# Key-side sums of a random-feature attention with the values stationary, in column halves

## The reference, cut to what matters

```python
logits = jnp.einsum('bhld,hdf->bhlf', k, W0) - 0.5 * jnp.sum(k * k, axis=-1, keepdims=True)
alpha = jax.nn.softmax(logits.reshape(B, H, L * NF), axis=2).reshape(B, H, L, NF)
N = jnp.einsum('bhlf,bhld->bhfd', alpha, v)      # the key-side sums
D = jnp.sum(alpha, axis=2)                       # their denominators
phi = jax.nn.softmax(jnp.einsum('bhld,hdf->bhlf', q, W0), axis=-1)
num = jnp.einsum('bhlf,bhfd->bhld', phi, N)
den = jnp.einsum('bhlf,bhf->bhl', phi, D)
out = num / (den[..., None] + EPS)
```

## Time and profile before

| | |
|---|---|
| median of 3 runs | 1093.77 us (1092.8 to 1097.36) |
| the profiled execution | 1093.86 us, of which the span 1092.1 |
| TensorE matmuls busy | 1010.6 us, 93% of the span |
| TensorE weight loads busy | 783.5 us, 72% |
| VectorE busy | 742.9 us, 68% |
| ScalarE busy | 451.5 us, 41% |
| GpSimd busy | 219.8 us, 20% |
| chain that ended last | TensorE 73%, VectorE 13%, issue 6%, ScalarE 3% |
| mean granted TensorE clock | 0.977 |

### The profile page before, as it was taken

How to read it: one execution, slowest core, us unless ns; L and a number is a source line. 1 busy time by engine, 2 the same in 40 slices (tenths; PEclk the granted TensorE clock), 3 DMA queues, 4 the chain that set the end, 5 groups by cost and what they waited for, 6 DMA issues and landing times.

```text
span 1092.1 us, 15333 instructions
## 1 busy us (share of the span) xinstructions
PE 1010.6 (93%) x5740; PEld 783.5 (72%) x5740; DVE 742.9 (68%) x1277; ACT 451.5 (41%) x757; POOL 219.8 (20%) x179
## 2 busy tenths in 40 slices
PE   6889999999999989889898998999999999899998
PEld 3568778887665556788874886888765556568898
DVE  5646677557466766888858385874665676677776
ACT  4414454020555565344333254521235465454442
POOL 6101211224311011223200022211360011021110
PEclk9988999999999999999999899999999999899999
DMA  6101000211000000010010000011110000001111
GB/s 210 43 20 40 1 1 1 58 38 41 20 1 1 1 1 1 20 40 20 21 58 1 20 20 1 2 27 52 39 39 1 1 1 1 0 1 40 27 32 40
DMA packets 12926, 26.75 MB, mean 24 GB/s; under 512 B 2581, under 2 KB 7285, under 8 KB 12853
## 3 DMA queue, kind: packets, MB, share of 16 engines
q1 hardware_dynamic: 12852, 25.77, 7.8%
HBM read 23.51 MB, written 2.10 MB: 23 GB/s over the span
## 4 chain that ended last, share of the span: by engine, by line
PE 73%; DVE 13%; issue 6%; ACT 3%; POOL 2%; SPq 2%; DMA 1%; DVEq 0%; ACTq 0%; POOLq 0%
PE ps L1204 14%; PE ps L897 13%; PE ps L1125 10%; PE ps L1085 4%; PE ps L1040 4%; PE ps L1101 3%; PE ps L1025 3%; PE ps L1169 3%; PE ps L905 3%; PE ps L1170 3%; DVE wide_lo L849 3%; PE ps L1154 2%; PE ps L1015 2%; PE ps L999 2%; SPq L264 2%
## 5 line engine op out<-in xcount | busy, mean ns | idle before, releaser
L1204 PE MATMUL ps<-expert_hi,wide_hi 128*128 128x256 f32 x512 | 148.0, 289 | 19.4 <-DVE wide_lo L849 19.3
L1125 PE MATMUL ps<-region 128*128 128x512 f32 (+3 forms) x384 | 163.9, 511 | 0.0
L777 DVE TENSOR_REDUCE region<-ps 128x1 f32<-128x512 f32 (+1 forms) x192 | 100.6, 552 | 91.1 <-PE ps L1104 90.3
L1204 PE MATMUL ps<-expert_lo,wide_hi 128*128 128x256 f32 x512 | 144.4, 282 | 0.0
L1204 PE MATMUL ps<-expert_hi,wide_lo 128*128 128x256 f32 x512 | 144.0, 281 | 0.0
L301 POOL TENSOR_TENSOR expert_lo<-expert,expert_hi 128x1024 fp32r<-128x1024 f32 x32 | 81.4, 2544 | 264.3 <-ACT expert_hi L402 264.0
L561 ACT ACTIVATE region<-ps 128x512 f32<-128x512 f32 x192 | 92.7, 488 | 97.1 <-PE ps L1172 63.9
L402 ACT ACTIVATE wide_hi<-region 128x512 fp32r<-128x512 f32 x128 | 80.2, 630 | 119.1 <-DVE region L834 118.6
L809 DVE COPY_PREDICATED region<-region,ps 128x512 f32<-128x512 uint32 x112 | 80.9, 735 | 62.9 <-PE ps L897 62.5
L1204 PEld LDWEIGHTS ps<-expert_hi,wide_hi 128*128 128x128 f32 x512 | 96.9, 189 | 31.1 <-DVE wide_lo L849 25.3
L834 DVE TENSOR_TENSOR region<-ps,region 128x512 f32<-128x512 f32 x128 | 87.9, 689 | 38.6 <-PE ps L1154 38.2
(11 more groups left out here) (141 smaller groups left out, 1922.1 us busy)
## 6 DMA issues: line engine op xcount, KB each, us to landing
expert<-in_value_experts SPq DMA_DIRECT2D x16, 512.0 KB, 3.7
expert<-in_output_experts SPq DMA_DIRECT2D x16, 512.0 KB, 3.6
out<-X SPq DMA_DIRECT2D x8, 256.0 KB, 2.4
X<-in_x SPq DMA_DIRECT2D x2, 512.0 KB, 4.6
X<-in_x SPq DMA_DIRECT2D x1, 1024.0 KB, 9.9
W<-in_W SPq DMA_DIRECT2D x1, 512.0 KB, 7.0
expert<-in_W3q SPq DMA_DIRECT2D x1, 512.0 KB, 3.5
expert<-in_W3k SPq DMA_DIRECT2D x1, 512.0 KB, 3.5
```

The lines of the kernel that those rows point to most:

```text
L777: dve.tensor_reduce(mx[:, i, at_mx:at_mx + 1], ps[:, max_bank(h, m), 0:w], AX.X, ALU.max).then_inc(sem["s_max"], 1)
L1125: mm(ps[:, SUM_BANK[c], lo:CH], V3[:, j, h // 2, h % 2 * HD3:(h % 2 + 2) * HD3], PT[:, g % RING, lo:CH], start=(j == 0), stop=(j == TC * ( ...
L1204: last = mm(ps[:, 4 + t // 2, t % 2 * D:(t % 2 + 1) * D], r[:, m % MO, k * P:(k + 1) * P], w[:, g % SLOTS, p * D:(p + 1) * D], start=(n == ...
```

## The change

The two operands change places. For a pair p and tile t, 64 columns of `V1_all` (the pair's 34 and what follows them) are stationary and the 128 columns of `E1` move. The result is transposed: values on partitions, features along the row. Even pairs go to partitions 0 to 63 of bank 4, odd pairs to 64 to 127 (`v` in the code), alternating tile by tile, so all 8 pairs fit in one bank. ScalarE copies that bank to `N1T` once both halves are done (`n_sb`), ahead of the first copy to `phT`. In step 2, behind the transposes of tile 1, TensorE transposes it back with four transposes (`nT_ps`, bank 5); VectorE copies from there to `N1w`, now with 6 copies (three runs of pairs with the same window offset, two head positions), behind the max and subtraction of tile 2. L1006's products and L695's additions follow, each moved behind other work of their step.

```diff
--- before.py
+++ after.py
@@ -130,6 +130,8 @@
         k_max = view(H1)
 
         N1w = view(PAIRS1 * WIN).rearrange("p (k w) -> p k w", k=PAIRS1)
+        at[0] = 0
+        N1T = view(CH)
         at[0] = 5 * 1024
         cx = view(2 * D).rearrange("p (i n) -> p i n", i=2)
         cxT = view(2 * DA * P).rearrange("p (i a s) -> p i a s", i=2, a=DA)
@@ -168,7 +170,7 @@
             var_ready=3 * TT, rstd_ready=3 * TT, xn_ready=3 * TT, xnT_ps=3 * TT, xT_ready=3 * TT, bias_added=2 * TT,
             k_ps=2 * NC, k_sb=2 * NC, q_ps=2 * NC, q_sb=2 * NC, v_ps=TT, v_sb=TT, kk_sb=1, kk_ps=1,
             fk_ps=TT, mk_ready=DA * TT, fk_sub=TT, e_ready=TT, ak_top_ready=1, k_max_ready=1, ak_ready=1, w_ready=1, wv_ready=1,
-            n_ps=2, n_blk=2 * PAIRS1, za_ps=1, n_ready=3,
+            n_ps=2, n_sb=1, nT_ps=1, n_blk=6, za_ps=1, n_ready=3,
             f_ps=2 * TT, top_ready=2 * TT * DA, f_sub=2 * TT, f_exp=2 * TT, fT_ps=2 * TT, fT_sb=2 * TT,
             num_ps=2 * TT, cx_ready=2 * TT, cxT_ps=2 * TT, cxT_sb=2 * TT, y_ps=2 * TT,
             q2_ps=2 * NC, q2_sb=2 * NC,
@@ -468,10 +470,11 @@
                 for s in range(LAST):
                     if s in (2, 3):
                         piece_high(b, s - 2)
+                    if s == 1:
+                        until(act, "n_ps", b, 2)
+                        copy(N1T, ps[:, 4, :], "n_sb")
                     for a, t in due(s, 1):
                         until(act, "fT_ps", b, a * TT + t + 1)
-                        if a + t == 0:
-                            until(act, "n_ps", b, 2)
                         if t >= 2:
                             until(act, "num_ps", b, a * TT + t - 1)
                         i = t % 2
@@ -688,12 +691,6 @@
                 for s in range(LAST):
                     if s - 2 in GATES_AT:
                         gates(GATES_AT.index(s - 2))
-                    if s == 2:
-                        until(dve, "za_ps", b, 1)
-                        for k0, k1, w0 in N1_RUNS:
-                            dens = N1w[:, k0:k1, w0 + HD1:w0 + 2 * V1W:V1W]
-                            dve.tensor_tensor(dens, dens, ps[:, 6, 2 * k0:2 * k1].rearrange("p (a i) -> p a i", i=2),
-                                              ALU.add).then_inc(sem["n_ready"], 1)
                     for a, t in due(s, 0):
 
                         i = t % 2
@@ -713,17 +710,21 @@
                                                      m[:, q].unsqueeze(3).broadcast_to([P, 2, H // 4, F]),
                                                      ALU.subtract)
                         last.then_inc(sem["f_sub"], 1)
-                    if s == 1:
-
-                        until(dve, "n_ps", b, 2)
+                    if s == 2:
+
+                        until(dve, "nT_ps", b, 1)
                         until(dve, "windows_clear", b, 1)
-                        for k in range(PAIRS1):
-                            w0 = k * 2 * V1W - N1_at(k)
-                            n1 = ps[:, 4 + k // 4, k % 4 * P:k % 4 * P + 2 * V1W]
-                            dve.tensor_copy(N1w[0:HALF, k, w0:w0 + V1W], n1[0:HALF, 0:V1W]
+                        nT = ps[:, 5, :].rearrange("p (k w) -> p k w", w=HALF)
+                        for k0, k1, w0 in N1_RUNS:
+                            dve.tensor_copy(N1w[0:HALF, k0:k1, w0:w0 + V1W], nT[0:HALF, k0:k1, 0:V1W]
                                             ).then_inc(sem["n_blk"], 1)
-                            dve.tensor_copy(N1w[HALF:P, k, w0 + V1W:w0 + 2 * V1W], n1[HALF:P, V1W:2 * V1W]
+                            dve.tensor_copy(N1w[HALF:P, k0:k1, w0 + V1W:w0 + 2 * V1W], nT[HALF:P, k0:k1, V1W:2 * V1W]
                                             ).then_inc(sem["n_blk"], 1)
+                        until(dve, "za_ps", b, 1)
+                        for k0, k1, w0 in N1_RUNS:
+                            dens = N1w[:, k0:k1, w0 + HD1:w0 + 2 * V1W:V1W]
+                            dve.tensor_tensor(dens, dens, ps[:, 6, 2 * k0:2 * k1].rearrange("p (a i) -> p a i", i=2),
+                                              ALU.add).then_inc(sem["n_ready"], 1)
                     for a, t in due(s, 2):
 
                         i = t % 2
@@ -1000,12 +1001,6 @@
                                           W0[r, i, cols_of] if a == 0 else kblk[r, b, i, cols_of],
                                           start=True, stop=True)
                         last.then_inc(sem["f_ps"], 1)
-                    if s == 2:
-                        until(pe, "n_blk", b, 2 * PAIRS1)
-                        for k0, k1, w0 in N1_RUNS:
-                            last = mm(ps[:, 6, 2 * k0:2 * k1], eps_blk,
-                                      N1w[:, k0:k1, w0 + HD1:w0 + 2 * V1W:V1W], start=True, stop=True)
-                        last.then_inc(sem["za_ps"], 1)
                     for a, t in due(s, 1):
                         until(pe, "f_exp", b, a * TT + t + 1)
                         until(pe, "fk_sub", b, TT)
@@ -1015,15 +1010,27 @@
                             last = pe.transpose(ps[0:r, k // TC, k % TC * P:(k % TC + 1) * P],
                                                 phi[:, t % 2, k * P:k * P + r], ident)
                         last.then_inc(sem["fT_ps"], 1)
+                    if s == 2:
+                        until(pe, "n_sb", b, 1)
+                        for u in range(PAIRS1 // 2):
+                            last = pe.transpose(ps[:, 5, u * P:(u + 1) * P], N1T[:, u * P:(u + 1) * P], ident)
+                        last.then_inc(sem["nT_ps"], 1)
+                        until(pe, "n_blk", b, 2 * len(N1_RUNS))
+                        for k0, k1, w0 in N1_RUNS:
+                            last = mm(ps[:, 6, 2 * k0:2 * k1], eps_blk,
+                                      N1w[:, k0:k1, w0 + HD1:w0 + 2 * V1W:V1W], start=True, stop=True)
+                        last.then_inc(sem["za_ps"], 1)
                     if s < 2:
 
                         until(pe, "e_ready", b, TT)
                         until(pe, "wv_ready", b, 1)
-                        for p in range(s * PAIRS1 // 2, (s + 1) * PAIRS1 // 2):
+                        for u in range(s * PAIRS1 // 4, (s + 1) * PAIRS1 // 4):
                             for t in range(TT):
-                                c0 = (t * PAIRS1 + p) * 2 * V1W
-                                last = mm(ps[:, 4 + p // 4, p % 4 * P:p % 4 * P + WIN], E1[:, t, p * P:(p + 1) * P],
-                                          V1_all[:, c0:c0 + WIN], start=(t == 0), stop=(t == TT - 1))
+                                for v in range(2):
+                                    c0, p = (t * PAIRS1 + 2 * u + v) * 2 * V1W, 2 * u + v
+                                    last = mm(ps[v * HALF:(v + 1) * HALF, 4, u * P:(u + 1) * P],
+                                              V1_all[:, c0:c0 + HALF], E1[:, t, p * P:(p + 1) * P],
+                                              start=(t == 0), stop=(t == TT - 1))
                         last.then_inc(sem["n_ps"], 1)
                     for a, t in due(s, 2):
                         until(pe, "fT_sb", b, a * TT + t + 1)
```

## The result

The changed kernel takes 1077.39 us (median of 4 runs, 1075.85 to 1080.7), the kernel before 1094.17 us (4 runs, 1092.8 to 1097.36). The ratio is 0.9847, with a 95% interval of 0.9815 to 0.9878: faster by 1.5%, 16.8 us. The forecast was 1081 with a range of 1077 to 1096 and 0.68 for "faster". The direction and the mechanism held; the gain is 4 us larger than the 12.6 us of the sum.

What follows compares the result with a forecast made beforehand. The key-side sums on TensorE were taken to lie nearly all on the path. From 1093.9 us, 14.2 less for paired records and 1.6 more for the handover gave 1081.3, say 1081 us, range 1077 to 1096.

Steps and rivals of the forecast that it cites:

- the sum: Whole kernel: 14.2 us saved on the key-side sums, 1.6 lost at the handover, from 1093.9 to 1081.3 us.
- What bounds the stage: Key-side sums (L1025) lie nearly all on the path, about 33 us of the 1092.1 us span.
- What a record cost before: Second half of L1025: 0.113 us each, paced by the 128-column weight load, not the 102 moving columns.
- Two halves at the same time: Key-side sums: records in different column halves overlap, 0.0575 us each; second half 3.7 us, saving 3.5 per batch.
- The first rival: Key-side sums: column halves don't overlap, 0.107 to 0.113 us per record; total near 1095 us; chance 0.21.
- the 0.090 of the short group: Key-side sums only partly paired: 0.090 us per record, as in a short row-half group; total 1087.2 us; chance 0.08.
- 15.1 us for perfect pairs: Key-side sums: saving if each record costs 0.053 us, half of 107 ns.
- Bare loads: Key-side sums: loads come into the open and halves don't overlap, 0.163 us per record; total 1108.5 us; chance 0.08.
- The first halves: First 64 records of the sums per batch: 6.0 and 6.7 us, saving 3.6 each, slow time kept at 4.9 and 6.3.
- The handover: From T (start of L999 after the sums) to next L999: 10.0 us against 9.2, +1.6 in all.

Runs made afterwards that it cites:

- experiment 5: The kernel before with 34 or 68 moving columns instead of 102: 1116.42 us beside 1089.54, and 1107.29 us beside 1096.69.
- thin_load: The changed kernel with 34 stationary columns instead of 64 for seven of the eight tiles: 1079.49 us beside 1092.52 for the kernel before.
- filler: The changed kernel with two unused float32 matmuls in TensorE's idle time before the first half of the sums: 1075.59 us beside 1096.69 for the kernel before.
- same_half: The changed kernel with all key-side sums on output partitions 0 to 63, odd pairs in bank 5: 1091.71 us beside 1089.54 for the kernel before.
- Experiment 6: The changed kernel again, 1077.75 us, and with the way back ahead of tile 1's transposes and tile 2's max, 1075.98 us.
- even_only: The changed kernel without the odd pairs' sums but for their first tile, 36 records per half: 1072.53 us beside 1089.54 for the kernel before.

## Why the prediction was right, point by point

*What bounds the stage.* Right. The sums lay on the path: 15.88 us in the stage, 16.0 at the end, though that match is closer than the parts outside the stage (+1.0, +0.5 and -1.6 us) give a right to. I had expected these parts unchanged.

*What a record cost before.* Right: the moving columns don't set the 0.113 us. With 34 and 68 instead of 102 the records cost the same at the same clock (experiment 5). That it is the load is what is left; no run shortened the load alone in the old form.

*Two halves at the same time.* Right, shown from both sides: 7.13 us without different halves, 3.64 for 36 records as for 64. The first rival predicted a second half of 6.9 to 7.2; it is exactly what the kernel does once the halves are the same. The term was 3.7 us against 3.64 measured. The row halves of the earlier trace rows were the right row to lean on, and the 0.090 of the short group was too careful. But row halves don't "pair perfectly", as the rivals have it: in the earlier trace rows the 8 records take 1.07 us, and perfect pairs would be half of the 1.71, 0.85. The loads came out shorter, as foretold: a median of 137 ns at L1031 and 192 at L1047, which loads 128 columns. The 15.1 us for perfect pairs is 14.9 when added up again; no bound of the range hangs on that 0.2.

*Bare loads.* Wrong rival: two records on one half take 0.222 us together and a pair on two halves 0.114, and the shorter load of `thin_load`, 34 columns instead of 64, changed nothing, so the loads are hidden. The Trainium skill ("TensorE: Matmul & The Clock Gate", "What overlaps and what doesn't") says that a load overlaps a matmul in flight only when it goes to other rows. This case doesn't bear that out, since all rows are shared here.

*The first halves: the step that was mis-sized.* I took 6.0 and 6.7 us, by keeping the slow time of before, 4.9 and 6.3 us, as it was. Measured are 5.31 and 5.08, 2.3 us less in all. I had also said that the first half still begins at the low clock; in batch 0 it doesn't. L1031 in batch 0 by microsecond (the figure behind the two busy counts is the granted clock):

```profile
65.80:66.80 1.00, 0.98 (x18) 1.00 (x20) 1.00 0.00 0
66.80:67.80 1.00, 1.00 (x18) 1.00 (x15) 0.69 0.06 16
67.80:68.80 1.00, 1.00 (x13) 1.00 (x11) 0.50 0.00 0
68.80:69.80 1.00, 1.00 (x14) 1.00 (x12) 0.50 0.00 0
69.80:71.10 1.30, 1.30 (x18) 1.16 (x14) 0.70 0.00 0
```

The clock was high when the half began, fell, and was back before its end, 3.4 us low in all by these rows instead of 4.9. In batch 1 it was low from the start and for 3.0 us, instead of 6.3. TensorE had been idle for 3.41 us before either, so the length of that wait alone doesn't give the level. `filler` shows that the rest of the distance to 3.64 is clock and nothing else. `same_half` has about the same low time (3.4 us in each batch) without the column halves; so what I mis-sized seems to come with the other operands, and is no merit of the halves. That my sum missed it on the side of a larger gain is luck.

*The handover.* 1.0 us too dear: +1.6 expected, +0.60 measured. Its chain was right to a tenth: exp(1) lets L1010 start at T + 2.63 (I had 2.65), the copies begin at T + 4.2, L1020 at T + 5.63 (5.7), L1047 at T + 6.95 (7.0 to 7.8). The low clock caught L1047 in batch 0 only (3.31 us for 16 records) and not in batch 1 (2.00), while I had counted half of it in both. Experiment 6 makes the handovers 3.0 and 1.7 us shorter; less 1.3 of clock in the first, the order had 1.7 us in it in each.

*A cost that I had left out.* The step from L1010 to L1031 grew by 0.09 us, from 0.93 to 1.02. The Trainium skill ("TensorEngine Tiling (Array Packing)", "Key Properties") says that changing the tiling mode drains the engine. The row fits that, at less than 0.1 us each time, but no run here isolates it.

So the sum was -14.2 + 1.6 = -12.6, and the rows gave -16.66 + 0.18 + 0.60 = -15.88. Of the difference of 3.3 us, 2.3 are the first halves, 1.0 the handover and 0.2 the second halves, less 0.2 for the steps between.

What stays open: why the clock is low for 4.9 and 6.3 us in the first halves of before and for 3.4 and 3.0 after. It isn't steady between variants either: in `thin_load` the first half of batch 0 takes 6.27 us, in `even_only` 3.61. The runs show what TensorE did before and what level was granted; a rule that would give the length isn't shown by them.

## What to carry to other kernels

When a matmul's useful output is at most 64 columns wide, try making that side stationary and putting two such products on the two output halves, alternating one by one in program order. Here, in float32 with 34 or 64 stationary and 128 moving columns, the second came free, but in groups of 16 records most of that was lost. Before that, look at what sets the pace of a record (load or moving columns), since trimming the one that is hidden gave nothing here, and with 34 and 68 moving columns it cost the clock. And look at the handover that such a transposed result needs: here 1.7 us per batch of it were set by where it stood in each engine's order, not by its few instructions.

## What the runs showed of the hardware that I had not expected

- Fewer moving columns made the kernel slower. With 34 instead of 102 columns per load-bound record, the granted clock was at 0.50 through 13.6 us of uninterrupted matmuls, and the program took 1116.42 us instead of 1089.54. With 68 it was 1107.29 beside 1096.69.
- 36 records and 64 records in 3.64 us: a matmul in the other column half is free to the hundredth of a microsecond.
- Around a change of half TensorE overlaps more than one record of the old and the new half (6.00 us for the grouped order, where 6.5 to 6.9 was expected).
